# Projecting h ahead of the neighbour sum, with adjacency blocks as the stationary operand

## The reference, cut to what matters

```python
def _sage(x, adj, Wr, Wx, b, mf):
    deg = jnp.clip(jnp.sum(adj, axis=-1, keepdims=True), 1.0, None)
    agg = jnp.einsum('bij,bjd->bid', adj, x) / deg
    out = agg @ Wr + x @ Wx + b
    nrm = jnp.maximum(jnp.linalg.norm(out, axis=-1, keepdims=True), NORM_EPS)
    return out / nrm * mf[..., None]
...
adj_d = _dilate(adj, mask)
h1 = _bn(jax.nn.relu(_sage(x, adj_d, Wr1, Wx1, b1, mf)), g1, be1)
h2 = _bn(jax.nn.relu(_sage(h1, adj_d, Wr2, Wx2, b2, mf)), g2, be2)
```

## Time and profile before

| | |
|---|---|
| median of three executions | 2655.53 us (2654.55 to 2658.29) |
| the profiled execution, its own time | 2651.22 us |
| its span in the profile | 2649.4 us |
| PE busy over the span | 2563.9 us, 97% |
| VectorE, ScalarE, GpSimd busy | 2083.7, 1369.0, 604.5 us |
| mean granted clock of PE, of full speed | 0.994 |

### The profile page before, as it was taken

The page is one execution under the profiler, slowest core; times in us unless marked ns, Lnnn a source line. Parts: engine busy times, 40 slices in busy tenths (PEclk is TensorE's granted clock), DMA queues, the critical chain, the costliest instruction groups (busy, mean ns, idle before and its releaser), DMA issues. The chain is left out here.

```text
span 2649.4 us, 38841 instructions
## 1 busy us (share of the span) xinstructions
PE 2563.9 (97%) x12390; PEld 1634.8 (62%) x12390; DVE 2083.7 (79%) x5413; ACT 1369.0 (52%) x4060; POOL 604.5 (23%) x265
## 2 busy tenths in 40 slices
PE   6999999999999999999999999999999999999998
PEld 4666666666656666666666654555555555554898
DVE  5778899999889889999888978666666645765776
ACT  4666656666635757557566312233332344443676
POOL 0000000000000000000000005766666604442672
PEclk9999999999999999999999999999999999999999
DMA  7354173463286364354371433555555329995763
GB/s 235 82 166 133 56 197 110 96 196 101 72 244 183 92 188 136 65 169 127 69 210 45 120 122 137 204 206 207 206 204 202 119 104 399 406 402 230 263 235 138
DMA packets 267637, 455.46 MB, mean 172 GB/s; under 512 B 152096, under 2 KB 152480, under 8 KB 263712
## 3 DMA queue, kind: packets, MB, share of 16 engines
q1 hardware_dynamic: 230560, 385.75, 43.0%
q10 hardware_dynamic: 36864, 67.13, 8.4%
HBM read 352.13 MB, written 67.11 MB: 158 GB/s over the span
## 5 line engine op out<-in xcount | busy, mean ns | idle before, releaser
L738 PE MATMUL a_acc<-a_ew,a_Hr 128*128 128x512 f32 x1536 | 750.0, 599 | 0.0
L918 DVE TENSOR_TENSOR a_ew<-adj,a_cos 128x512 f32<-128x512 f32 x768 | 506.8, 680 | 56.3 <-PE a_cos L731 54.9
L729 PE MATMUL a_cos<-a_nh 128*128 128x512 f32 x768 | 418.7, 545 | 17.1 <-DVE a_nl L910 9.4
L738 PEld LDWEIGHTS a_acc<-a_ew,a_Hr 128*128 128x128 f32 x1536 | 274.5, 189 | 157.4 <-issue 113.3
L855 ACT ACTIVATE a_v<-a_D,a_wb,a_small 128x256 f16<-128x256 f32 x512 | 288.4, 634 | 141.1 <-PE a_D L771 86.1
L658 POOL TENSOR_TENSOR a_Au<-a_Ab,tri 128x512 fp8e4<-128x512 fp8e4 x32 | 36.2, 1132 | 1337.1 <-ACT a_Ab L838 1337.1
L731 PE MATMUL a_cos<-a_nh,a_nl 128*128 128x512 f32 x768 | 304.1, 396 | 0.0
L730 PE MATMUL a_cos<-a_nl,a_nh 128*128 128x512 f32 x768 | 301.4, 392 | 0.0
L1418 PE MATMUL b_acc<-adj,b_z 128*128 128x512 f32 x512 | 225.0, 592 | 0.0
L1515 PE MATMUL b_acc<-adj,b_z 128*128 128x512 f32 x512 | 222.5, 592 | 0.0
L1755 POOL TENSOR_TENSOR b_dsum<-adj 128x1024 f32<-128x1024 f32 x15 | 133.3, 8886 | 380.0 <-DVE adj L1663 380.0
(11 more groups left out here) (267 smaller groups left out, 4375.4 us busy)
## 6 DMA issues: line engine op xcount, KB each, us to landing
adj<-in_adjT SPq DMA_DIRECT2D x108, 1024.0 KB, 12.5
stage<-in_adj ACTq DMA_DIRECT2D x256, 256.0 KB, 3.1
adj<-in_adjT SPq DMA_DIRECT2D x128, 512.0 KB, 4.2
scr_keep<-a_T SPq DMA_DIRECT2D x32, 512.0 KB, 3.2
scr_z<-b_zT SPq DMA_DIRECT2D x32, 512.0 KB, 3.6
scr_ag<-b_a SPq DMA_DIRECT2D x32, 512.0 KB, 3.1
stage<-scr_keep SPq DMA_DIRECT2D x13, 1024.0 KB, 6.7
b_kp<-scr_keep SPq DMA_DIRECT2D x12, 1024.0 KB, 6.7
```

Of the source, the lines that this page charges most:

```text
L729: e.matmul(cos[j][:], n[:, blk(k)], n[:, half(j)], start=True, stop=False)
L738: e.matmul(acc[j][:], Hr[u % 2][:, k, :], ew[idx % EW][:], start=(k == 0), stop=(k == NK - 1)).then_inc(E["agg"], 1)
L918: e.tensor_tensor(ew[idx % EW][:], adj[g % 2][:, k, half(j)], cos[j][:], ALU.mult).then_inc(E["ew"], 1)
```

## The change

h is multiplied by the neighbour weights first, and the adjacency sums the product: (adj h) Wr becomes adj (h Wr). In the new `agg_h` a block of 128 x 128 of the masked adjacency is stationary and 129 columns stream: 128 of the product and a column of ones, whose sum is the degree. The results come out unturned (nodes x features) in `third`, three banks made of p1 and half of pt, each with up to three groups of 129 columns. That is 64 multiplications per graph in place of 16 of 512 columns. The product h Wr is written by PE to p2 (`project_r`) and copied by ScalarE into `mix` (`keep_r`), which takes over the memory of `dsum`. The root product (`project_x`) and its weights stay. aT, its copies, GpSimd's and VectorE's additions and the degree multiplications are gone; VectorE copies the degree columns out of PSUM. The masks of a graph are made in two groups of four, on either side of the scaled additions. z's sum keeps its form, and turning z stands in the middle of its second half. Both turned h and turned z now go through p2, as do both projections. Both weights are loaded ahead, in the first stage (`W1`).

```diff
+        C["W1"] = sb("W1", [128, 2, 128])
...
+                    if g == 2:
+                        e.wait_ge(E["w"], 32)
+                        e.dma_start(C["W1"][:], A["W"][:, 3:5, :]).then_inc(E["w"], 16)
...
+            e.wait_ge(E["w"], 48)
...
+        deg, dg, gate = P.sb("deg", [128, NK]), P.sb("dg", [128, NK]), P.sb("gate", [128, 1])
+        mix = dsum[:].rearrange("p i n -> p (i n)")[:, 0:NK * 129].rearrange("p (k c) -> p k c", c=129)
...
+        third = [flat2(p1)[:, 0:512], flat2(p1)[:, 512:1024], flat2(pt)[:, 0:512]]
...
+        def sums(k, first, last):
+            return third[k // 3][:, 129 * (k % 3) + first:129 * (k % 3) + last]
...
+            def load_adj(n):
                 if n > 2:
-                    e.wait_ge(E["ag"], 2 * use_z(n - 3) + 2)
-                    e.wait_ge(E["ds"], 7 * (n - 2))
-                if n > 1:
-                    for c in range(4):
-                        e.dma_start(adj[n % 3][:, 2 * c:2 * c + 2, :],
-                                    adj_rows(A, ORDER[n])[:, 2 * c:2 * c + 2, :]).then_inc(E[f"adj{n % 3}{c}"], 16)
+                    e.wait_ge(E["az"], 2 * (n - 3) + 2)
+                for c in range(4):
+                    e.dma_start(adj[n % 3][:, 2 * c:2 * c + 2, :],
+                                adj_rows(A, ORDER[n])[:, 2 * c:2 * c + 2, :]).then_inc(E[f"adj{n % 3}{c}"], 16)
...
             for n in range(1, G + 1):
                 m = n - 1
+                if n + 2 < G:
+                    load(n + 2)
...
                 if n + 2 < G:
-                    load(n + 2)
+                    load_adj(n + 2)
...
+            def agg_h(n):
+                if n:
+                    e.wait_ge(E["f"], 8 * n)
+                else:
+                    e.wait_ge(E["on"], 1)
+                e.wait_ge(E["m"], n + 1)
+                for q in range(NK):
+                    e.wait_ge(E["mk"], 8 * n + q + 1)
+                    for k in range(NK):
+                        t = e.matmul(sums(k, 0, 129), adj[n % 3][:, q, blk(k)], mix[:, q, :], start=(q == 0 and k % 3 == 0),
+                                     stop=(q == NK - 1), skip_group_check=True)
+                t.then_inc(E["ah"], 1)
+
+            def agg_z(m, j, blocks=range(NK)):
+                if blocks[0] == 0:
+                    e.wait_ge(E["zr"], m + 1)
+                    if m:
+                        e.wait_ge(E["ev"], 2 * (m - 1) + j + 1)
                 for q in blocks:
-                    if j == 0:
-                        e.wait_ge(E["mk"], 8 * n + q + 1)
-                    t = e.matmul(acc[j][:], src[:, q, :], adj[n % 3][:, q, half(j)], start=(q == 0),
...
+            def turn_h(n):
+                if n:
+                    e.wait_ge(E["hr"], n)
+                    e.wait_ge(E["c"], n)
+                for k in range(NK):
+                    t = e.transpose(p2[:, k, :], h[n % 2][:, k, :], C["ident"][:])
+                t.then_inc(E["th"], 1)
+
+            def turn_z(m):
                 e.wait_ge(E["zr"], m + 1)
-                e.wait_ge(E["c"], m + 1)
+                if m < G - 2:
+                    e.wait_ge(E["m"], m + 3)
+                else:
+                    e.wait_ge(E["c"], G)
+                    e.wait_ge(E["zt"], m)
                 for k in range(NK):
                     t = e.transpose(p2[:, k, :], z[m % 2][:, k, :], C["ident"][:])
                 t.then_inc(E["tz"], 1)
...
+            def project_r(n):
+                e.wait_ge(E["hT"], n + 1)
+                for k in range(NK):
+                    t = e.matmul(p2[:, k, :], hT[:, blk(k)], C["W1"][:, 0, :], start=True, stop=True)
+                t.then_inc(E["pm"], 1)
+
+            def project_x(n):
+                if n > 1:
+                    e.wait_ge(E["zt"], n - 1)
+                else:
+                    e.wait_ge(E["m"], n + 1)
+                for k in range(NK):
+                    t = e.matmul(p2[:, k, :], hT[:, blk(k)], C["W1"][:, 1, :], start=True, stop=True)
+                t.then_inc(E["pr2"], 1)
+
+            turn_h(0)
+            project_r(0)
+            project_x(0)
+            for n in range(G):
+                agg_h(n)
+                if n + 1 < G:
+                    turn_h(n + 1)
...
+                    agg_z(n - 1, 0)
+                if n + 1 < G:
+                    project_r(n + 1)
...
+                    agg_z(n - 1, 1, range(HALF))
+                    turn_z(n - 1)
+                    agg_z(n - 1, 1, range(HALF, NK))
+                if n + 1 < G:
+                    project_x(n + 1)
...
+            turn_z(G - 1)
+            agg_z(G - 1, 0, range(6))
             fold1_pe(e)
-            agg(*last, 0, range(early, NK))
+            agg_z(G - 1, 0, range(6, NK))
             project_a(0)
             project_z(0)
-            agg(*last, 1)
+            agg_z(G - 1, 1)
...
+            def keep_h(n):
                 e.wait_ge(E["th"], n + 1)
                 if n:
                     e.wait_ge(E["pr2"], n)
-                e.activation(hT[:], flat2(p1), ACT.Copy).then_inc(E["hT"], 1)
+                e.activation(hT[:], flat2(p2), ACT.Copy).then_inc(E["hT"], 1)
+
+            def keep_r(n):
+                e.wait_ge(E["pm"], n + 1)
+                if n:
+                    e.wait_ge(E["ah"], n)
+                e.activation(mix[:, :, 0:128], p2[:], ACT.Copy).then_inc(E["m"], 1)
+
+            keep_h(0)
+            keep_r(0)
+            for n in range(G):
                 if n + 1 < G:
                     ln(n + 1)
+                    keep_h(n + 1)
+                if n > 1:
+                    e.wait_ge(E["az"], 2 * (n - 2) + 2)
+                scales(n, E, "f")
+                if n + 1 < G:
+                    keep_r(n + 1)
                 if n:
+                    keep_a1(n - 1, 0)
                     keep_z(n - 1, E, p2)
...
+                    keep_a1(n - 1, 1)
...
                     e.tensor_tensor(*masked(b, c, q), ALU.mult).then_inc(E["mk"], 1)
+
+            def root(n):
+                e.wait_ge(E["pr2"], n + 1)
+                if n > 1:
+                    e.wait_ge(E["zr"], n - 1)
+                elif n == 0:
+                    e.wait_ge(E["wl"], 48)
+                e.tensor_tensor(o[n % 2][:], p2[:], over_rows(C["rows"][:, 3, :]), ALU.add).then_inc(E["c"], 1)
...
+            e.memset(mix[:, :, 128:129], 1.0).then_inc(E["on"], 1)
+            e.memset(C["onesf"][:], 1.0)
+            masks(0, range(NK))
+            norm(1)
             e.tensor_tensor(C["mf2"][:], C["mf"][:], C["mf"][:], ALU.mult)
+            root(0)
             for n in range(G):
+                g = ORDER[n]
                 if n + 1 < G:
-                    prep(n + 1)
-                if n:
...
+                    if n:
+                        norm(n + 1)
+                    masks(n + 1, range(HALF))
+                e.wait_ge(E["ah"], n + 1)
+                for i in range(3):
+                    many = min(3, NK - 3 * i)
+                    e.tensor_copy(deg[:, 3 * i:3 * i + many],
+                                  third[i][:, 0:129 * many].rearrange("p (k c) -> p k c", c=129)[:, :, 128]).then_inc(E["deg"], 1)
+                e.wait_ge(E["deg"], 3 * n + 3)
+                e.tensor_scalar(dg[:], deg[:], 1.0, None, ALU.max).then_inc(E["dgm"], 1)
...
-                e.tensor_tensor(C["rho"][:, g, :], dp, C["rdeg"][:, g, :], ALU.mult).then_inc(E["dgc"], 1)
...
                 e.wait_ge(E["c"], n + 1)
                 for k in range(NK):
-                    e.scalar_tensor_tensor(o[n % 2][:, k, :], p1[:, k, :], C["rdeg"][:, g, k:k + 1],
+                    e.scalar_tensor_tensor(o[n % 2][:, k, :], sums(k, 0, 128), C["rdeg"][:, g, k:k + 1],
                                            o[n % 2][:, k, :], ALU.mult, ALU.add).then_inc(E["f"], 1)
+                e.tensor_tensor(C["rho"][:, g, :], deg[:], C["rdeg"][:, g, :], ALU.mult).then_inc(E["dgc"], 1)
+                if n + 1 < G:
+                    masks(n + 1, range(HALF, NK))
                 unit_norm(n, E)
                 e.tensor_tensor(rm[:], rn[:], col8(C["mf"], g), ALU.mult).then_inc(E["rm"], 1)
+                if n:
+                    moments(n - 1, E, stats[0])
+                if n + 1 < G:
+                    root(n + 1)
             moments(G - 1, E, stats[0])
...
-            for n in range(1, G):
...
+            e.wait_ge(E["zt"], G)
+            e.memset(gate[:], 0.0)
```

More of the change, by code:

```diff
@@ L1485, in project_a @@
                 else:
-                    e.wait_ge(E["ev"], 2 * use_z(G - 2 + p) + 2)
+                    e.wait_ge(E["ev"], 2 * (G - 2 + p) + 2)
                 if p:
@@ L1494, in project_a @@
                 t.then_inc(F["pr1"], 1)
-            turn(G - 1)
-            last, early = (G - 1, z[(G - 1) % 2], use_z(G - 1)), 6
-            agg(*last, 0, range(early))
+            turn_z(G - 1)
+            agg_z(G - 1, 0, range(6))
             fold1_pe(e)
-            agg(*last, 0, range(early, NK))
+            agg_z(G - 1, 0, range(6, NK))
```

(13 more changed lines are left out.)

113 lines of the change are left out of this document (11 added, 102 removed).

## The result

The changed kernel takes 2646.18 us (median of 8 runs, 2639.58 to 2648.14), the kernel before 2655.04 on the same chip (8 runs, 2653.63 to 2658.29). The medians differ by 8.9 us, a ratio of 0.9967. The ratio on record, which is not that of the medians, is 0.9956, 95% interval 0.9946 to 0.9966, or 9.0 to 14.3 us less. So the changed kernel is faster, by 8.9 us as the medians have it and rather more by the ratio. The forecast was 2648.5, in a range from 2640 to 2658. The profiled execution took 2643.41 us, of which 2641.4 is its span.

A forecast was written before the change was run, and what follows sets the result against it. PE's own instruction stream was taken to bound the steady part. Steady graphs save 16.0 us, the shorter end 6.2, the start loses 15.2: 7.0 less, so 2655.5 becomes 2648.5 us, range 2640 to 2658.

The forecast's parts named there:

- rival 1: New `agg_h` passes paced by the weight load, 0.107 us each: 11 us more gain, 2637 us; chance 0.08.
- rival 2: New `agg_h` passes go at 0.117 us each: 9.5 us less gain, 2658 us, no measurable change; chance 0.12.
- rival 5: Weight loads in `agg_h` run serially: 13.7 us more per graph, total near 2867 us; chance 0.01.
- The small operations: VectorE's two operations on rnss and rnrn, ahead of `keep_r`, fall to 0.17 us once GpSimd's additions go.
- A: End of a graph's `agg_h`; `keep_r` forecast to end about 12.1 us later, PE reaching z's turning at 12.96.
- the slow rival: Turning of z waits for `keep_r` as small operations stay long: PE waits 2.8 us per graph, 2691 us; chance 0.10.
- The start: Second stage's first graphs, from 1591.6: half-clock projections, then PE idle 8.25 us before `project_x(1)`; loses 15.2 us.
- A0: End of the first graph's neighbour sum, `agg_h(0)`, forecast at about 1617.5 us.
- A1: End of `agg_h(1)`, forecast at 1648.3 us, including 2.5 us for half clock after the idle stretch.
- The end: Stage's last stretch, from last neighbour sum to last turning of z: forecast 14.6 us against 20.85, saving 6.2.
- A15: End of the last graph's neighbour sum, forecast at 2116.3 us after 14 beats of 33.43 us.
- rival 4: Start worse than charged: 5 us more half clock in each of two first sums, 2653.5 us; chance 0.09.

The follow-up runs named there:

- before_thin_adds: Kernel before, with GpSimd's degree additions cut to 8 columns in all graphs but the first: 2653.63 us against 2652.97, ratio 0.9996.
- before_no_degrees_again: Kernel before without its 16 one-column degree passes per graph, degrees replaced by stand-ins from SBUF, repeated in rounds: 2638.6 us against 2657.24, ratio 0.993.
- after_adds_back: Changed kernel with GpSimd's additions put back over 1000 columns, results unread, for each graph but the first: 2719.52 us in one run.
- before_no_degrees: Kernel before without its 16 one-column degree passes per graph, stand-ins read from SBUF, single run: 2641.32 us against 2652.97.
- after_delay_1: Changed kernel with one extra VectorE multiplication of 1024 columns per graph ahead of `unit_norm`: 2650.71 us in one run.
- after_delay_3: Changed kernel with three extra VectorE multiplications of 1024 columns per graph ahead of `unit_norm`: 2711.2 us.
- the early copy: Changed kernel with `keep_r(1)` moved ahead of the scaling of z of graph 0 on ScalarE: 2635.51 us, ratio 0.9923 to before.

## Why the prediction was right

- **What binds.** Right. PE's own stream sets the steady part before and after: no group of it has idle time ahead, and `before_thin_adds` shows that freeing GpSimd and VectorE there is worth nothing.
- **The pace of the 128 passes.** Forecast 0.1123 a pass, measured 0.1117; beat 33.43 against 33.35. Neither end of the range came. The floor of the one-column passes (rival 1) was not reached at 128 or 129 columns. The 0.117 of the neighbour weights (rival 2) was not their own pace: with the degree passes ahead taken out, the same group takes 1.79 (1915.85 to 1917.64, in `before_no_degrees_again`), so 0.08 of its 1.87 came from what stood before it. The prediction's new sum has them at 1.79 without a reason; that proved right.
- **Serial loads** (rival 5). Wrong, as rows 3 and 4 said: 14.29 us hold 128 loads and 128 passes. The sentence of the Trainium skill that the prediction draws on stands in another section (TensorE: Matmul & The Clock Gate, "The mechanism"): weight loads overlap matmuls in flight only when they aim at another row group. The trace disagrees with it, since all loads here use the full array. The same section also lets a load go ahead when it is aimed at a background buffer for weights, which the prediction left out. These rows fit that, though no run here shows which buffer a load went to.
- **The small operations.** Right: 0.16 and 0.17 (L1699, L1741) after the change. `keep_r` ended at A + 11.9, forecast A + 12.1; the slack was 1.1, forecast 0.8. The mechanism of the slow rival is real, since `after_adds_back` gives A + 16.3 against its 15.7. Its price was wrong in two terms, which did not matter as the rival did not come. The wait was 3.4 us per graph and not 2.8, and the clock's fall behind it, put at nothing, cost 2.0 more on average. Built, it took 2719.52 where the rival said 2691. The rival's threshold does not follow from its own terms either: with one wait in each of 14 graphs and the same at the start, a gain of 7.0 is used up at 1.2 us of lateness, not 1.7.
- **The start.** Forecast 25.9 (1591.6 to 1617.5). Measured 25.9 from VectorE's first instruction of the stage (1594.17 to 1620.06), and 26.3 from PE's first transposes at 1593.77, where the forecast's terms begin. The terms that it shows add up to 24.0 to 25.6, so some 0.3 of the 25.9 is not accounted for there. The granted clock was back at 1607, 13 us after PE began, and not after 3.2 as in the earlier trace rows; the forecast came near because it had taken the projections at half clock. Idle 7.74 against 8.25. From A0 to A1 30.47 against 30.8, with half clock as charged.
- **The end.** From A15 = 2117.43 to the last turning 14.61, forecast 14.6.
- **The sum.** From VectorE's first instruction to the last turning: forecast 539.3, measured 537.9. 1.1 us of the difference are the 14 beats of 0.08, and the rest is the start. Inside the trace the stage gained 8.4 where 7.0 was forecast: 17.1 for 16.0 in the steady graphs, 6.2 as forecast at the end, 14.9 for 15.2 lost at the start. So the number is right because its parts are, and not because errors cancel. The gain of 7.0 is still somewhat small: the medians differ by 8.9, and the interval of the ratio starts at 9.0.
- **What was left out of account.** The prediction calls a first or third stage that changes length a sign of being wrong. In the profile the first stage ended 2.55 us later, and the stretch behind the last turning took 509.4 us for 511.5. Both lie within what executions of one kernel or kernels with the same code there differ by (3.4 and 4.5 us; 508.2 to 512.4 us over all profiles), so they are no effect of the change. That they nearly cancel here is luck, and it need not be so: the single run of `before_no_degrees` gained 7 us less than the median of `before_no_degrees_again`.

That rival 4 did not come holds for the runs made, and why is not shown. The clock came back at different places of the first projections: `project_x(0)` took 3.78 in the profile after and 2.05 in `after_delay_1`. What decides that is open. It is worth up to 1.8 us (3.58 against 1.89 from start to start).

## What to carry to other kernels

Turning a product round, so that the small operand streams and the large one is stationary, is to be costed by passes of a row with the same shape, and here that row, 1.78 us for 16, was right to 0.4%. Then look for the buffer that the new order makes two engines share: its slack in the steady part decided between 9 us gained and 67 lost (`after_adds_back` against before), and at the start, where no other graph's work covers it, it cost 9 us, which one line moved gave back. A wait of PE is to be priced with the slower clock that can follow it, and a single run is best read by the length of the changed stage. A stand-in in an experiment should read from the same memory as what it replaces.

## What the runs showed of the hardware that was not expected

- **The granted clock can fall after a short idle stretch.** The prediction tied the half clock to idle stretches of 8 us. Idle of 2.56 us (`after_delay_3`) and 3.29 us (`after_adds_back`) in a beat that is otherwise all busy was also followed by 0.50. On top of the wait itself it cost 1.5 to 1.7 us per graph in the first kernel and up to 3.0 in the second. It does not always come: behind the longest of those waits, 3.62 us ahead of 2133.66 in `after_adds_back`, the granted clock stayed 1.00 and nothing was lost. What decides that is open. Behind the wait of 1.11 us in the early copy, from 1623 to 1624, the granted clock was 1.00.
- **The time of a group holds a part of its neighbour.** The same 16 passes took 1.87 us behind one-column passes and 1.79 behind 512-column passes.
- **129 columns and 128 cost the same**, 14.29 and 14.30 us for 128 passes.
- **A stalled small operation, and which ones.** With GpSimd adding 1000 columns beside them, the operations L1702 and L1744 over 8 columns took 2.28 and 1.92 us, alone 0.16 and 0.17. The reciprocal between them took 0.20 in every run. The degree operations of the kernel before, which read PSUM, took 0.16 and 0.17 beside the additions; reading `dsum` in SBUF they took 2.32 and 2.21 (`before_no_degrees`). The 0.17 of `before_thin_adds` says nothing of additions over 8 columns beside it: there they had ended at 1928.51, 8 us ahead of the operation.
